# Softmax's maximum as the bias of four exponentials, a residual chain behind the next maximum, and pad copies spread over three steps

## The reference

```
x = x + tanh(g_xattn) * attention(layernorm(x), ctx)
    # q = rope(ln(x) @ Wq), k, v = ctx @ Wkv, k = rope(k)
    # softmax(q k^T / 4) v per head, then @ Wout + bout
x = x + tanh(g_ffn) * moe(layernorm(x))
    # probs = softmax(h @ gate^T), top 6, not renormalised
    # sum over the 6 of prob * (silu(h w1g) * (h w1u)) w2, plus the shared expert
```

## Time and profile before

| | us |
|---|---|
| median of 3 runs | 1695.9 |
| the runs | 1713.83, 1695.52, 1695.9 |
| the profiled execution | 1689.32 |
| its span, first to last instruction | 1687.4 |
| mean granted clock of TensorE, of full | 0.896 |
| busy: PE, DVE, ACT, POOL | 1580.9, 726.4, 498.1, 671.3 |

### The profile page before, as it was taken

The page is one execution under the profiler, slowest core; times in us unless marked ns, Lnnn a source line. Parts: engine busy times, 40 slices in busy tenths (PEclk is TensorE's granted clock), DMA queues, the critical chain, the costliest instruction groups (busy, mean ns, idle before and its releaser), DMA issues.

```text
span 1687.4 us, 32240 instructions
## 1 busy us (share of the span) xinstructions
PE 1580.9 (94%) x9026; PEld 1334.5 (79%) x9027; DVE 726.4 (43%) x1527; ACT 498.1 (30%) x986; POOL 671.3 (40%) x1135
## 2 busy tenths in 40 slices
PE   4999999999999995499999999999999999989998
PEld 2666766766666663399999999999999999879997
DVE  4555665666565664122222222222222222245555
ACT  3333333433333341122232223222322232211111
POOL 4426533334333324044734344444433330454442
PEclk9777777777797885699999999999999999999999
DMA  4102311222111123433333333333333332265553
GB/s 170 68 29 68 119 67 66 77 92 97 66 66 66 58 77 124 153 125 95 123 127 133 133 127 127 133 133 127 127 134 133 127 127 83 86 188 187 184 180 113
DMA packets 76311, 190.54 MB, mean 113 GB/s; under 512 B 10497, under 2 KB 12546, under 8 KB 73570
## 3 DMA queue, kind: packets, MB, share of 16 engines
q1 hardware_dynamic: 54562, 99.81, 18.2%
q0 software_dynamic: 21696, 90.06, 15.2%
HBM read 117.07 MB, written 72.76 MB: 113 GB/s over the span
## 4 chain that ended last, share of the span: by engine, by line
PE 56%; POOL 1%; SPq 1%; DVE 1%; issue 1%; DMA 0%; ACT 0%; DVEq 0%; POOLq 0%
PE bank L1322 32%; PE bank L1352 18%; PE bank L1293 3%; PE bank L1333 3%; POOL w_lo L209 0%; SPq L1144 0%; SPq L1145 0%; POOL gath L1238 0%; POOL w_lo L220 0%; DMA gath<-y_rows,y_slots 0%; DVE tree L1417 0%; POOL w_hi L205 0%; DMA xr<-expert_rows 0%; POOL w_hi L217 0%; SPq L1148 0%
## 5 line engine op out<-in xcount | busy, mean ns | idle before, releaser
L1322 PE MATMUL bank<-w_hi,x_hi 128*128 (+1 forms) x1152 | 293.0, 336 | 1.6 <-POOL w_lo L209 1.6
L1322 PE MATMUL bank<-w_lo,x_hi 128*128 (+1 forms) x1152 | 280.4, 324 | 0.0
L1322 PE MATMUL bank<-w_hi,x_lo 128*128 (+1 forms) x1152 | 280.2, 324 | 0.0
L205 POOL CAST w_hi<-w_raw 128x352 fp32r<-128x352 f32 x144 | 62.5, 486 | 468.6 <-PE bank L1322 468.6
L1408 DVE SCALAR_TENSOR_TENSOR act<-silu,row_w,bank 128x352 f32<-128x352 f32 x112 | 65.0, 580 | 325.2 <-ACT silu L1265 311.2
L1265 ACT ACTIVATE silu<-bank 128x352 f32<-128x352 f32 x144 | 67.0, 465 | 460.4 <-PE bank L1322 460.4
L1322 PEld LDWEIGHTS bank<-w_lo,x_hi 128*128 128x128 f32 x1152 | 202.5, 189 | 0.0
L1322 PEld LDWEIGHTS bank<-w_hi,x_lo 128*128 128x128 f32 x1152 | 202.0, 189 | 0.0
L1322 PEld LDWEIGHTS bank<-w_hi,x_hi 128*128 128x128 f32 x1152 | 195.6, 190 | 1.8 <-POOL w_lo L209 1.8
L638 PE MATMUL bank<-k_t,q_t 32*128 32x256 f32 x512 | 186.0, 493 | 1.7 <-ACT k_t L559 1.4
L1352 PE MATMUL bank<-w_hi,a_hi 128*128 (+3 forms) x432 | 172.9, 400 | 6.9 <-DVE a_lo L1396 5.7
(11 more groups left out here) (184 smaller groups left out, 2508.6 us busy)
## 6 DMA issues: line engine op xcount, KB each, us to landing
xr<-expert_rows SPq DMA_DIRECT2D x112, 264.0 KB, 2.7
y_rows<-y SPq DMA_DIRECT2D x112, 256.0 KB, 2.0
w_raw<-in_w POOLq DMA_DIRECT2D x18, 1408.0 KB, 6.9
w_raw<-in_w POOLq DMA_DIRECT2D x18, 512.0 KB, 8.1
x_sb<-in_x SPq DMA_DIRECT2D x16, 256.0 KB, 2.7
x_res<-in_x SPq DMA_DIRECT2D x16, 256.0 KB
x_rows<-x SPq DMA_DIRECT2D x16, 256.0 KB, 3.7
x_rows<-row SPq DMA_DIRECT2D x16, 256.0 KB, 3.8
```

The lines of the kernel that those rows point to most:

```text
L1322: last = nc.tensor.matmul(to[:, 0:WIDTH], xx[jt][:, d, :], w[d][half][:, cols], start=(d == 0 and xx is x_hi and w is w1_hi), stop=(d == D ...
```

## The change

Three edits, in one diff.

1. ACT takes the maximum in. DVE scales the four maxima of a group by -SCALE (128 x 4) and no longer subtracts them. ACT reads the scores where PE wrote them, and does one exponential per head, 128 x 128, with the scaled maximum of that head as its bias. The bank of the scores is thus in use until `exp_done`, for which the scores and the maximum of two groups later wait; `soft` is written by ACT, which waits for the transposes of two groups before.
2. On DVE, the residual and its statistics (new function `residual`) come behind the maximum of group 4, and the normalised row behind that of group 6. The bias addition stays ahead.
3. On SP, the pad copies of experts 4 to 15 are issued four at a time in steps 0, 1 and 2 of phase_b, behind the load of tile 2 and of each next one, instead of all at the head.

```diff
--- before.py
+++ after.py
@@ -520,7 +520,11 @@
                 if at(ATTEND):
                     b = at(ATTEND)[0]
                     act.wait_ge(shifted, b * GROUPS + u + 1)
-                    a.activation(soft[u % 2][:], soft[u % 2][:], ACT.Exp, scale=SCALE).then_inc(exp_done, 1)
+                    need(act, prob_mm, b * GROUPS + u - 1)
+                    for h in range(4):
+                        last = a.activation(soft[u % 2][:, h, :], bank[2 + u % 2][:, h * P:(h + 1) * P], ACT.Exp,
+                                            bias=smax[u % 2][:, h:h + 1], scale=SCALE)
+                    last.then_inc(exp_done, 1)
                 of, v = earlier(at, u, 1)
                 if of:
                     b = of[0]
@@ -632,7 +636,7 @@
                         pe.wait_ge(kt_done, 2 * (b + 1))
 
                     r = 32 * (u % 4)
-                    need(pe, shifted, b * GROUPS + u - 1)
+                    need(pe, exp_done, b * GROUPS + u - 1)
                     for c in range(2):
                         ch = 2 * (u // 4) + c
                         last = nc.tensor.matmul(bank[2 + u % 2][:, c * 2 * P:(c + 1) * 2 * P],
@@ -874,11 +878,10 @@
             def attend(u, b, j, n):
                 dve.wait_ge(score_mm, b * GROUPS + u + 1)
                 s3 = bank[2 + u % 2][:].rearrange("p (h n) -> p h n", h=4)
+                need(dve, exp_done, b * GROUPS + u - 1)
                 v.tensor_reduce(smax[u % 2][:], s3, AX.X, ALU.max).then_inc(smax_done, 1)
                 dve.wait_ge(smax_done, b * GROUPS + u + 1)
-                need(dve, prob_mm, b * GROUPS + u - 1)
-                v.tensor_tensor(soft[u % 2][:], s3, smax[u % 2][:, :, None].to_broadcast([P, 4, P]), ALU.subtract)\
-                    .then_inc(shifted, 1)
+                v.tensor_scalar(smax[u % 2][:], smax[u % 2][:], -SCALE, None, ALU.mult).then_inc(shifted, 1)
 
             def normalised_row(b, j, n):
                 dve.wait_ge(var2, b + 1)
@@ -917,16 +920,19 @@
                 if u == 4:
                     dve.wait_ge(o_mm, b + 1)
                     ch.step(v.tensor_tensor(proj, bank[1][:], bout_b[:], ALU.add))
-                    ch.sync()
-                    dve.wait_ge(res_in, 16 * (b + 1))
-                    need(dve, x1_out, 16 * b)
-                    v.scalar_tensor_tensor(out=x1[:], in0=proj, scalar=tanh2[:, 0:1], in1=x_res[:],
-                                           op0=ALU.mult, op1=ALU.add).then_inc(x1_done, 1)
-                    dve.wait_ge(x1_done, b + 1)
-                    ch.step(v.bn_stats(stats2[:], x1[:]))
-                    ch.sync(passed_v)
-                    v.bn_aggr(mean2[:], stats2[:]).then_inc(var2, 1)
-                    ch.end()
+
+            def residual(b, j, n, ch):
+                ch.sync()
+                dve.wait_ge(res_in, 16 * (b + 1))
+                need(dve, x1_out, 16 * b)
+                v.scalar_tensor_tensor(out=x1[:], in0=proj, scalar=tanh2[:, 0:1], in1=x_res[:],
+                                       op0=ALU.mult, op1=ALU.add).then_inc(x1_done, 1)
+                dve.wait_ge(x1_done, b + 1)
+                ch.step(v.bn_stats(stats2[:], x1[:]))
+                ch.sync(passed_v)
+                v.bn_aggr(mean2[:], stats2[:]).then_inc(var2, 1)
+                ch.end()
+
             def gate(u, b, j, n, ch):
                 if u == 0:
                     dve.wait_ge(x2_hi_done, b + 1)
@@ -1032,10 +1038,12 @@
                 for u in range(GROUPS):
                     if at(TAIL) and u in (3, 4):
                         tail(u, *at(TAIL), ch)
+                    if at(ATTEND):
+                        attend(u, *at(ATTEND))
+                    if at(TAIL) and u == 4:
+                        residual(*at(TAIL), ch)
                     if at(TAIL) and u == 6:
                         normalised_row(*at(TAIL))
-                    if at(ATTEND):
-                        attend(u, *at(ATTEND))
                     if at(TAIL) and u == 2:
                         tail(u, *at(TAIL), ch)
                     if at(PROJECT):
@@ -1175,14 +1183,18 @@
             for e in range(2):
                 sp.dma_start(rows[EXPERTS * CAP + e * BLOCK:EXPERTS * CAP + (e + 1) * BLOCK, :], pad_row[:])\
                     .then_inc(pads_out[0], 16)
-            pads(range(4, EXPERTS))
 
             def one_step(i, at):
                 if i == 0:
                     load(2, 0, 1)
+                if i is not None and i < 3:
+
+                    pads(range(4 * i + 4, 4 * i + 8))
                     sp.wait_ge(pads_out[0], 16 * 6)
-                    for k in range(1, EXPERTS // 4):
-                        sp.wait_ge(pads_out[k], 16 * 4)
+                    if i > 0:
+                        sp.wait_ge(pads_out[i], 16 * 4)
+                if i == 3:
+                    sp.wait_ge(pads_out[3], 16 * 4)
                 if live(i, -2) and routed(i, -2):
                     store(*at(-2))
                 if i is None or starts_tile(i, 1):
```

## The result

| | before | after |
|---|---|---|
| median, us | 1697.22 (4 runs) | 1641.01 (4 runs) |
| from, to, us | 1695.52, 1713.83 | 1636.36, 1645.52 |
| the profiled execution, us | 1689.32 | 1645.52 |
| granted clock | 0.896 | 0.929 |

What follows compares the result with a forecast made beforehand. TensorE, often at its lower clock, was taken to bound the first stage. From the profiled 1689.3 us, 85 (first stage) and 10 (pads) come off: 1594, or 1601 us against the median; range 1573 to 1650.

Steps and rivals of the forecast that it cites:

- the remark on transposes: Groups 4 to 7: transposes don't count as busy, so the clock cannot hold; rival at 1668 us, chance 0.05.

Runs made afterwards that it cites:

- e4: The changed kernel with DVE's scaling over five columns instead of four, the fifth a zero that nobody reads; 1605.3 us, ratio 0.947.
- e9: The changed kernel with four transposes of the unit matrix on PE in group 7, ahead of the wait for the exponential; ratio 0.934.
- e10: The changed kernel with two 128 x 512 matmuls on PE in group 7, ahead of the wait for the exponential; ratio 0.938.
- e5: The changed kernel with the scaling of the four maxima moved from DVE to ACT, in front of its four exponentials; ratio 0.939.
- e3: The changed kernel without DVE's scaling: -SCALE goes into the copy of the projected queries, a minimum replaces the maximum; 1571.5 us, ratio 0.927.
- e11: e3 with two 128 x 512 matmuls added on PE in group 7, ahead of the wait for the exponential; 1568.2 us, ratio 0.927.

## What to carry to other kernels

Where TensorE's granted clock falls again and again at the same place, add up its idle time over that place, the waits too short to be listed among the big ones too, and try a filler there: four useless transposes, 0.66 us together, were worth 3% here, and they show in one run whether the waits cost their length or the clock. Before an operation on DVE is called free, follow each result behind it to its reader: 0.17 us eight times a round, and now and then a hold-up, decided between 0.965 and 0.927. A factor that is constant belongs in an instruction that exists already.

## What the runs showed of the hardware

- A 128x4 operation from SBUF to SBUF on DVE stood for 8.64 us while POOL went through a dozen instructions, and 6.93 to 6.98 us at the same place in e4, e9 and e10. This was rare: of 128, four were over 0.7 us. The other three ended at the end of a single POOL instruction (within 0.03 us), one of them (181.59 to 182.73) while POOL's run went on to 183.93. So it does not always wait for the whole run; why it got in nowhere from 139.24 to 147.88 stays open.
- Four transposes as a filler kept the clock at 1.00 as well as two matmuls did (e9, e10), against the remark on transposes that the prediction takes from the Trainium skill (TensorE: Matmul & The Clock Gate).
- The same wait of 0.58 us passed 5 times of 5 in e5 and cost 13.7 us of low clock in the changed kernel. How the idle times of groups 6 and 7 join in this stays open, as do the three falls with less than 0.5 us and those of 3.4 us behind the gate products, with PE busy throughout (after at 359.0, e3 at 238.0, e11 at 355.4).
